# Causal attention on one core: the second value projection moves in between the two output projections

## The reference

```python
qkv = jnp.einsum('bse,ehd->bshd', xn, qkv_w) + qkv_b
q, k, v = jnp.split(qkv, 3, axis=-1)
logits = jnp.einsum('bqhd,bkhd->bhqk', q, k) / jnp.sqrt(64)
mask = jnp.tril(jnp.ones((1024, 1024), dtype=jnp.bool_))
logits = jnp.where(mask, logits, large_negative)
probs = jax.nn.softmax(logits, axis=-1)
attn = jnp.einsum('bhqk,bkhd->bqhd', probs, v)
x = x + jnp.einsum('bqhd,hde->bqe', attn, out_w) + out_b + ffn(xn)
```

## Time and profile before

| What | Value |
|---|---|
| median of 3 runs | 1489.68 us (1490.0, 1484.68, 1489.68) |
| span of the profiled execution | 1484.0 us |
| PE busy | 1439.4 us, 97% of the span |
| DVE, ACT, POOL busy | 84%, 62%, 65% |
| 16 DMA engines, slices of the attention | 7 to 8 tenths busy |
| granted TensorE clock | 9 or more tenths in every slice |

### The profile page before, as it was taken

One profiled execution on the slowest core, in us unless ns is written; L12 is line 12 of the kernel. 1 busy time (PEld: TensorE's weight loads), 2 busy tenths in 40 slices (PEclk: granted clock), 3 DMA queues, 4 the chain that ended last, 5 costly groups with the idle time before them and its releaser, 6 DMA issues.

```text
span 1484.0 us, 26195 instructions
## 1 busy us (share of the span) xinstructions
PE 1439.4 (97%) x8770; PEld 880.5 (59%) x8770; DVE 1254.0 (84%) x1966; ACT 918.0 (62%) x1862; POOL 967.9 (65%) x752
## 2 busy tenths in 40 slices
PE   8989999999999999999999998889999999999998
PEld 6745555555555555555555555456667676776767
DVE  7587788788887888888888878479999999999997
ACT  4456666666666666666666766547665675657562
POOL 5144545546545556555456555539999999999895
PEclk9999999999999999999999999999999999999999
DMA  8058777777777777778777778500000000000000
GB/s 189 1 135 213 170 169 176 184 165 177 176 180 171 171 182 181 166 174 185 171 169 172 184 167 198 120 1 1 0 9 8 1 8 1 8 8 1 8 1 15
DMA packets 77136, 163.91 MB, mean 110 GB/s; under 512 B 31410, under 2 KB 43724, under 8 KB 77004
## 3 DMA queue, kind: packets, MB, share of 16 engines
q1 hardware_dynamic: 77004, 162.24, 47.5%
HBM read 9.08 MB, written 2.10 MB: 8 GB/s over the span
## 4 chain that ended last, share of the span: by engine, by line
PE 87%; DVE 5%; issue 3%; POOL 3%; ACT 2%; SPq 0%; DMA 0%; DVEq 0%; POOLq 0%; ACTq 0%
PE accum L1108 18%; PE both L1045 14%; PE both L2798 9%; PE misc L1012 8%; PE flips_all L1045 6%; PE flips_all L2821 5%; PE flips_all L1132 4%; PE misc L1022 4%; PE flips_all L2810 4%; PE flips_all L2858 2%; PE accum L2810 2%; PE both L1049 2%; PE flips_all L1049 2%; PE accum L2821 2%; PE flips_all L2844 1%
## 5 line engine op out<-in xcount | busy, mean ns | idle before, releaser
L451 POOL TENSOR_SCALAR big<-big,recip 128x384 f32<-128x384 f32 (+7 forms) x512 | 374.9, 747 | 431.8 <-DVE recip L719 431.7
L727 DVE STREAM_TRANSPOSE big<-big 128x896 f32<-128x896 f32 (+7 forms) x288 | 345.4, 1224 | 17.0 <-POOL big L451 16.3
L532 ACT ACTIVATE big<-both,neg_max 128x1024 f32<-128x1024 f32 (+3 forms) x256 | 243.3, 955 | 170.9 <-DVE neg_max L709 165.7
L1108 PE MATMUL accum<-across,v_sb 128*64 128x256 f32 (+1 forms) x2560 | 269.9, 361 | 13.4 <-issue 13.4
L709 DVE TENSOR_REDUCE neg_max<-both 128x1 f32<-128x1024 f32 (+3 forms) x256 | 248.3, 1011 | 21.5 <-PE both L1049 21.5
L1108 PEld LDWEIGHTS accum<-across,v_sb 128*64 128x64 f32 x2560 | 180.6, 137 | 131.9 <-issue 71.4
L1045 PE MATMUL both<-qk_sb 64*128 64x512 f32 (+3 forms) x1024 | 213.5, 534 | 3.9 <-ACT big L532 2.3
L532 ACT ACTIVATE big<-flips_all,neg_max 128x128 f32<-128x128 f32 (+3 forms) x256 | 131.9, 525 | 95.8 <-DMA across<-big 48.8
L2798 PE MATMUL both<-slow_sb,h_T 128*128 128x512 f32 x384 | 182.3, 602 | 7.4 <-DVE xnT L2311 4.0
L1607 POOL TENSOR_TENSOR prod<-xnT,qs 128x1024 f32<-128x1024 f32 (+3 forms) x32 | 180.2, 5638 | 12.2 <-DVE qs L2311 12.2
L1045 PEld LDWEIGHTS both<-qk_sb 64*128 64x128 f32 x1024 | 91.6, 186 | 112.6 <-issue 109.4
(11 more groups left out here) (224 smaller groups left out, 2368.6 us busy)
## 6 DMA issues: line engine op xcount, KB each, us to landing
across<-big SPq DMA_DIRECT2D x1024, 144.0 KB, 3.1
out<-x SPq DMA_DIRECT2D x8, 256.0 KB, 2.3
x<-in_L_attn_x SPq DMA_DIRECT2D x3, 512.0 KB, 5.6
slow_sb<-in_L_attn_w_slow SPq DMA_DIRECT2D x3, 512.0 KB, 7.6
w_qk<-in_L_attn_qkv_w SPq DMA_DIRECT2D x2, 512.0 KB, 6.5
xn<-in_L_ffn_W SPq DMA_DIRECT2D x1, 1024.0 KB
x<-in_L_attn_x SPq DMA_DIRECT2D x2, 256.0 KB, 2.9
qs<-in_L_attn_qkv_w SPq DMA_DIRECT2D x1, 512.0 KB, 6.1
```

Source lines behind the costliest of these rows:

```text
L451: pool.tensor_scalar(part, part, recip[:, u % 2, SLOTS.index(row), h:h + 1], 0.0, ALU.mult, ALU.add).then_inc(scaled, 1)
L532: last = act.activation(probs_of(row, h).rearrange("p b j k -> p j b k"), scores_of(row, h).rearrange("p (j b k) -> p j b k", b=MOVES, k=3 ...
L727: dve.transpose(part, part).then_inc(turned[group_of(row)], 1)
L1108: last = pe.matmul(dst, lhsT=values_of(u, j, h), rhs=keys_of(g, rows[n:n + 2], j, h), start=j == 0, stop=j == rows[n + 1])
```

## The change

In TensorE's `unit(u)`, `project_values(u + 1, 1)` moves up by one line, from behind both joins to between them:

```diff
@@ -1158,8 +1158,8 @@
                 score(u, 3)
                 project(u + 1, 1, 1)
                 join(u - 1, 0)
+                project_values(u + 1, 1)
                 join(u - 1, 1)
-                project_values(u + 1, 1)
 
             flip_xn(0)
             hidden(0, 0)
```

## The result

| Kernel | Median | Runs | Against the kernel before |
|---|---|---|---|
| before | 1486.28 us (1482.45 to 1490.04) | 20 | |
| changed | 1489.99 us (1487.18 to 1492.99) | 20 | ratio 1.0023, 95% interval 1.0015 to 1.0032 |

The changed kernel is slower by 3.7 us by the medians, 2 to 5 us by the interval. The forecast was 4.6 us slower.

The account below looks back on a forecast made before the run. TensorE's own list was taken as the bound, except in units with late transfers. A 0.33 us stall, paid fully in 13 units and partly in 3, gave 4.7 us, taken as 4.6: 1494.3 us, range 1488.5 to 1500.5.

Parts of the forecast that it names:

- all absorbed: Rival: TensorE waits for transfers in nearly every unit, so the 0.33 us stalls vanish: 1489.7 us; chance 0.15.
- within 0.5%: Chance 0.70 that the changed kernel's time differs from before by no more than 0.5%, about 7.4 us.
- The new wait: Value projection between the joins: TensorE waits for ScalarE's copy of bank 2, 0.33 us a unit, at most 0.39.
- What comes later: Behind the wait: next first scores load 3.2 us after the first join (2.86 before), L520's 0.21 us wait goes.
- The sum: Over 30 units: 13 pay 0.33 us, 3 pay part, 14 absorb it; together 4.7 us, taken as 4.6 on the median.
- Transfers come later too: Rival: group 0's later transfers delay group 1, so all 30 units pay: 9.9 us, 1499.6 us; chance 0.25.
- The rule of rotating banks: Skill rule that independent groups rotate through banks spoke against the new order; alone it would give 0, the rows 0.33 us.

Follow-up runs that it names:

- e1: Kernel before with the value projection after the first join and two matmuls of the second (12 passes of cover): 1486.93 us, ratio 1.0006.
- e2: Kernel before with the value projection after the first join and one matmul of the second (10 passes of cover): 1487.18 us, ratio 1.0006.
- e3: Kernel before with the value projection ahead of both joins (0 passes of cover): 1510.62 us, ratio 1.0170.
- e6: Kernel before with two more transfers of 129 KB in front of group 1's: 1529.00 us, ratio 1.0285.
- e7: Changed kernel with two more transfers of 129 KB in front of group 1's: 1527.66 us, ratio 1.0271 against the kernel before.
- e4: Kernel before with each transfer cut to three quarters of its columns from unit 1 on (output differs): 1475.57 us, ratio 0.9931.

## Why the prediction was right or wrong

- *Direction and size.* 4.6 us slower were forecast, 3.7 us measured (2 to 5 us). The forecast of 1494.3 us sat on a median of three runs that was 3.4 us too high; measured were 1489.99 us, which is outside the forecast's own range of 1491 to 1497 us. As an absolute time it lies next to the 1489.7 us of "all absorbed"; only against the runs of before made together with it is it the forecast's case.
- *The step that failed* is the statement that a measurement of this kernel can hardly tell 0.3% from no change ("about 0.5%, 7.4 us"), and with it the 0.70 for "within 0.5%", which amounts to calling it no change. No row gave that bound; there were three runs, which spread over 5.3 us. Twenty runs tell 0.23% from nothing with an interval of 0.17%. The slowdown that I had worked out was real and clear of noise, and the text should have said so.
- *The new wait*: 0.28 us on the loads and 0.31 us in the length of a unit, against 0.33 us (at most 0.39). Its release, 0.05 us behind the copy, was as read. e1, e2 and e3 show it shrink and grow with the cover by 0.11 to 0.12 us a pass.
- *What comes later*: as forecast. The first scores load at 3.20 us; L520's wait is gone; nothing came of it.
- *The sum*: charged 29 x 0.31 = 9.0 us, of which 4.4 us were left in the two profiled executions; forecast 4.7 us for 30 units. So 4.6 us were taken up, 5.2 us in the forecast. The waits of L1108 in ordinary units fell from 7.6 us in 15 to 8.9 - 1.15 - 2.81 = 4.9 us in 10 (the two subtracted are the first and the last of the window, at 137.82 and 930.41), where I had said about 3 us. One of the two long waits that the sum lets absorb the stall, the one at 924.33 us, didn't shrink (2.55 us before, 2.81 us after). The price is a mean over chance: which units are late differs between executions. I also read the 5.7 us between the median and the profile's span as possible waiting; each timed execution of the later runs is 1.7 to 1.9 us longer than its core's span, so only about 4 us could be that.
- *All absorbed* is what e6 and e7 show when every unit is late; it wasn't this kernel's case. *Transfers come later too*: group 0 did start 0.3 us later, but didn't take group 1 along. The landings of group 1 in the changed kernel (19.54 us by the median, 19.48 before) show it; e3 bears it out with a longer stall, and e7 excludes the full price. The reason given against it, that a longer unit keeps the distance, was argued, not tested by itself.
- *The rule of rotating banks* (Trainium skill, "Perfetto Trace Analysis", "Matmuls") named the right risk and gave no size: what matters is when the copy ends (1.20 us after the first join's load), not how long it takes (0.69 us). Cover beyond that point made no difference: 12 passes did as well as 16 (e1).

## What to carry to other kernels

When an engine that is full works through one bank several times, measure the time from the last use to the end of the copy, with what stands ahead of the copy in its engine's list, and keep that much other work in between; more is no use and less is paid pass by pass. Where a second loop, here the transfers, runs at nearly the same length as the first, a delay is paid only in the rounds where the second is early: count rounds, don't multiply. And if some rounds wait for the second loop, look there for the gain: the end of a chain cut in two gave 6 us, which none of the orders tried here did.

## What was not expected of the hardware

The 16 transfers of a group go out 0.64 us apart at either of two sizes. SyncE's issues for one group, before (144 KB each) and in e4 (108 KB each):

```profile
529.96 10.23 SPq L358 DMA_DIRECT2D across<-big  x16
```

```profile
525.68 10.28 SPq L359 DMA_DIRECT2D across<-big  x16
```

A quarter less to move saved nothing of the 10.2 us of issuing, only the landing at its end (median 3.1 us before, 2.2 us in e4). That fits the 0.9 us, and not 3, by which e4's group 1 was earlier.

The stretch ahead of the first join (115.6 to 118.5 us) and that behind the thirtieth (579 to 582 us) differ by that much between the profiles of before, the changed kernel and the experiments with their transfers as they are, whose orders there are nearly or wholly the same. A difference of spans between two profiles of this kernel below some 5 us says nothing; the length of a unit that waits for no transfer repeats to 0.01 us.
